# Attention with batch normalisation: x and output channel-major, the last load cut in three, one weight load on ScalarE's queue

## The reference, cut to what matters

```python
q, k, v = (einsum('oc,bchw->bohw', W, x).reshape(16, 8, 16, 256) for W in (Wq, Wk, Wv))
k = softmax(k, axis=-2)                          # over the 16 channels of a head
context = einsum('bhdn,bhen->bhde', k, v)
out = einsum('bhdn,bhde->bhen', q, context).reshape(16, 128, 16, 16)
y = einsum('oc,bchw->bohw', Wo, out) + x
mean, var = y.mean((0, 2, 3)), y.var((0, 2, 3))  # per channel, over all images
return (y - mean) * rsqrt(var + 1e-5) * gamma + beta
```

## Time and profile before

| | |
|---|---|
| Median of 3 runs | 53.73 us (52.9 to 54.81) |
| Span of the profiled execution, first to last instruction | 51.0 us |
| The median over that span | 2.7 us more |
| Busy: TensorE, VectorE, ScalarE, GpSimd | 37.5, 34.3, 27.2, 18.6 us |
| HBM read, written | 2.36 MB, 2.10 MB |

### The profile page before, as it was taken

The page is one execution under the profiler, slowest core; times in us unless marked ns, Lnnn a source line. Parts: engine busy times, 40 slices in busy tenths (PEclk is TensorE's granted clock), DMA queues, the critical chain, the costliest instruction groups (busy, mean ns, idle before and its releaser), DMA issues.

```text
span 51.0 us, 1103 instructions
## 1 busy us (share of the span) xinstructions
PE 37.5 (74%) x377; PEld 32.5 (64%) x377; DVE 34.3 (67%) x90; ACT 27.2 (53%) x61; POOL 18.6 (37%) x28
## 2 busy tenths in 40 slices
PE   3999997892789799999999999999999700000000
PEld 3999996681877498888888979797969600000000
DVE  0028699923999986994996799763764989991000
ACT  3633918509799991494386179827246926500000
POOL 5820075974994989843016008180000000000000
PEclk9999999999999999999999999999999999995555
DMA  0499999700000000000000000000000000599993
GB/s 0 121 217 360 242 295 366 241 11 0 0 0 13 0 0 0 0 6 0 0 13 6 0 0 0 0 0 13 0 0 0 0 0 0 170 338 337 343 343 113
DMA packets 4741, 4.52 MB, mean 89 GB/s; under 512 B 384, under 2 KB 4736, under 8 KB 4736
## 3 DMA queue, kind: packets, MB, share of 16 engines
q1 hardware_dynamic: 4736, 4.46, 27.7%
HBM read 2.36 MB, written 2.10 MB: 87 GB/s over the span
## 4 chain that ended last, share of the span: by engine, by line
PE 47%; DVE 16%; DMA 14%; SPq 6%; issue 3%; ACT 2%; DVEq 1%; ACTq 0%
DMA x_sb<-x_dram 14%; PE banks L505 10%; PE banks L432 9%; PE banks L472 9%; PE banks L457 8%; PE banks L489 7%; DVE y_sb L413 6%; SPq L218 4%; PE banks L486 3%; DVE stats L386 3%; DVE k_max L341 3%; DVE k_sum L354 1%; ACT x_hi L282 1%; SPq L222 1%; DVEq L64 1%
## 5 line engine op out<-in xcount | busy, mean ns | idle before, releaser
L269 POOL TENSOR_TENSOR probs<-probs,k_inv 128x256 f32<-128x256 f32 (+1 forms) x11 | 8.9, 823 | 9.2 <-DVE k_inv L360 9.2
L261 POOL TENSOR_TENSOR x_lo<-x_sb,x_hi 128x512 fp32r<-128x512 f32 (+1 forms) x7 | 7.9, 1129 | 5.5 <-ACT x_hi L282 5.5
L432 PE MATMUL banks<-wkv_hi,x_hi 128*128 128x256 f32 x32 | 7.2, 309 | 1.4 <-ACT v_sb L293 1.4
L282 ACT ACTIVATE x_hi<-x_sb 128x256 fp32r<-128x256 f32 (+1 forms) x11 | 5.4, 512 | 5.3 <-DMA x_sb<-x_dram 5.2
L341 DVE TENSOR_REDUCE k_max<-banks 128x16 f32<-128x256 f32 (+1 forms) x11 | 5.7, 529 | 1.8 <-PE banks L432 1.7
L354 DVE TENSOR_REDUCE k_sum<-probs 128x16 f32<-128x256 f32 (+1 forms) x11 | 5.6, 531 | 1.8 <-ACT probs L287 1.8
L303 ACT ACTIVATE a_hi<-banks 128x256 fp32r<-128x256 f32 (+1 forms) x9 | 3.3, 362 | 6.6 <-PE banks L489 6.6
L432 PE MATMUL banks<-wkv_hi,x_lo 128*128 128x256 f32 x32 | 6.5, 284 | 0.3 <-POOL x_lo L261 0.3
L432 PE MATMUL banks<-wkv_lo,x_hi 128*128 128x256 f32 x32 | 6.5, 287 | 0.0
L432 PEld LDWEIGHTS banks<-wkv_hi,x_hi 128*128 128x128 f32 x32 | 5.0, 196 | 2.2 <-ACT x_hi L282 1.5
L472 PE MATMUL banks<-w_sb,ct_sb 64*64 64x128 f32 x64 | 5.2, 281 | 0.5 <-DVE ct_sb L368 0.5
(11 more groups left out here) (42 smaller groups left out, 57.7 us busy)
## 6 DMA issues: line engine op xcount, KB each, us to landing
x_sb<-x_dram SPq DMA_DIRECT2D x1, 1024.0 KB, 7.1
out_dram<-y_sb SPq DMA_DIRECT2D x2, 512.0 KB, 3.5
x_sb<-x_dram SPq DMA_DIRECT2D x3, 256.0 KB, 3.2
out_dram<-y_sb SPq DMA_DIRECT2D x3, 256.0 KB, 3.5
x_sb<-x_dram SPq DMA_DIRECT2D x2, 128.0 KB, 2.2
w_sb<-w_dram SPq DMA_DIRECT2D x2, 128.0 KB, 3.0
out_dram<-y_sb SPq DMA_DIRECT2D x2, 128.0 KB, 2.0
gamma_beta<-affine_dram SPq DMA_DIRECT2D x1, 1.0 KB, 6.8
```

Of the source, the lines that this page charges most:

```text
L261: nc.gpsimd.tensor_tensor(x_lo[:, p, px], x_sb[:, p, px], x_hi[:, p, px].bitcast(F32), ALU.subtract).then_inc(x_lo_ready, hi - lo)
L269: nc.gpsimd.tensor_tensor(heads, heads, inv.to_broadcast([128, (hi - lo) * CH * HEADS, D]), ALU.mult).then_inc(probs_ready, hi - lo)
L282: nc.scalar.activation(x_hi[:, p, px], x_sb[:, p, px], ACT.Copy).then_inc(x_hi_ready, hi - lo)
L432: last = nc.tensor.matmul(kv_ps(p)[:, g, :], xs[:, p, g * 128:(g + 1) * 128], ws[:, :], start=start and g == CH * image, stop=stop, skip_g ...
```

## The change

In DRAM, x and the output become (channel, image, position); the host transposes them before and after. A load of several images is then one contiguous row for each channel: 2 KiB for two images, 4 KiB for four, and rows of one load lie 16 KiB apart. The same holds for the stores. The load of images 8 to 15 becomes (8,10), (10,12) and (12,16), each with a semaphore of its own. The key/value weights are issued by ScalarE, as the first instruction of its program, and the query/output weights behind the fifth load of x. No instruction that computes is changed.

```diff
-        x_landed = [sem(f"x_landed{i}") for i in range(6)]
+        x_landed = [sem(f"x_landed{i}") for i in range(8)]
...
-        PIECES = [(0, 1), (1, 2), (2, 4), (4, 6), (6, 8), (8, 16)]
+        PIECES = [(0, 1), (1, 2), (2, 4), (4, 6), (6, 8), (8, 10), (10, 12), (12, 16)]
...
             for i, (lo, hi) in enumerate(PIECES):
-                sp.dma_start(x_view[:, lo:hi, :], x[lo:hi].rearrange("b c n -> c b n")).then_inc(x_landed[i], 16)
-                if i == 0:
-                    sp.dma_start(w_sb[:, 0:2 * C], w[:, 0:2 * C]).then_inc(wkv_landed, 16)
-                if i == 3:
+                sp.dma_start(x_view[:, lo:hi, :], x[:, lo:hi, :]).then_inc(x_landed[i], 16)
+                if i == 4:
                     sp.dma_start(w_sb[:, 2 * C:4 * C], w[:, 2 * C:4 * C]).then_inc(wqo_landed, 16)
...
-                sp.dma_start(out[lo:hi].rearrange("b c n -> c b n"), y_view[:, lo:hi, :]).then_inc(stored, 16)
+                sp.dma_start(out[:, lo:hi, :], y_view[:, lo:hi, :]).then_inc(stored, 16)
...
         @block.scalar
         def _(act):
+            act.dma_start(w_sb[:, 0:2 * C], w[:, 0:2 * C]).then_inc(wkv_landed, 16)
...
-        "x_dram": np.ascontiguousarray(x).reshape(B, C, N),
+        "x_dram": np.ascontiguousarray(x.reshape(B, C, N).transpose(1, 0, 2)),
...
-    args.append(nc.dram_tensor("out_dram", (B, C, N), F32, kind="ExternalOutput").ap())
+    args.append(nc.dram_tensor("out_dram", (C, B, N), F32, kind="ExternalOutput").ap())
...
-    return result.results[0]["out_dram"].reshape(shape)
+    return result.results[0]["out_dram"].transpose(1, 0, 2).reshape(shape)
```

## The result

The changed kernel takes 50.89 us (median of 4 runs, 50.75 to 51.0) where the kernel before took 53.31 (4 runs, 52.87 to 54.81). The ratio is 0.958, with a 95% interval of 0.950 to 0.967: 2.2 us faster (1.8 to 2.7). The profiled execution took 51.0 us with a span of 49.3, so 1.7 us lie around the span.

What follows compares the result with a forecast made beforehand. Loads bound the front (one late load of images 8 to 15), TensorE the middle, VectorE's last outputs and stores the end. 1.6 + 0.5 + 0.5 = 2.6 us off 53.73 gives 51.1, range 50.1 to 52.8.

Steps and rivals of the forecast that it cites:

- The stages: Whole kernel: loads, TensorE run, stores have different limits; the 25 us between 17.14 and 42.5 carry over unchanged.
- The split, 1.6: Front: ScalarE's wait for images 8 and 9 goes, they land at 9.05 at the latest; TensorE run starts 1.6 us earlier.
- The issues that move, 0.5: Early loads: the third load, issued 0.47 us sooner, moves VectorE's k_max row by 0.3 to 0.7; 0.5 us taken.
- The stores, 0.5: End of the kernel: wider rows in memory make the bare stores faster, near 381 GB/s, gaining 0.5 us.
- Rival 1: Stores: wide rows gain nothing, the engines write at 340 GB/s whatever the row; 51.6 us, chance 0.15.
- rival 4: Loads and stores: rows 16 KiB apart are served badly by HBM, for instance 230 GB/s; 55.5 us, chance 0.06.
- estimate of 0.3: Stores: from a fixed cost of about 3 cycles a packet beside 1 for 32 bytes, a gain of some 0.3 us.
- 3: Front: ScalarE's weight load goes behind its table load, TensorE starts 0.83 later, the 0.5 is gone; 51.7 us, chance 0.05.
- 5: Loads: each pays a fixed cost one after another, last images at 15.7, eating the front's 2.1; 53.5 us, chance 0.01.
- rival 2: Front: another wait replaces the sixth load's, about 0.9 of the front and some store gain left; 52.6 us, chance 0.13.
- a first VectorE cast later than 3.5: Start of the kernel: a sign of being wrong; the weights were expected to land at 3.0 to 3.4.
- a remaining wait for images 8 and 9: Front, ScalarE: a sign of being wrong; no wait for data past 7.5 us was expected.

Runs made afterwards that it cites:

- layout_only: The kernel before with only x and the output channel-major: 51.94 us, ratio 0.990 (0.976 to 1.004).
- weights_only: The kernel before with only the key/value weights on ScalarE's queue and the query/output weights behind the fifth load: 53.28 us, ratio 1.015 (1.002 to 1.027).
- store_layout_only: The kernel before with only the output channel-major: 51.97 us, ratio 0.971 (0.959 to 0.984).
- split_only: The kernel before with only the last load cut in three: 51.64 us, ratio 0.981 (0.971 to 0.991).
- changed_again: The changed kernel as it is, measured once more: 50.67 us (6 runs), ratio 0.964 (0.956 to 0.973) against the kernel before.
- no_layout: The changed kernel with the image-major layout of before, keeping split and moved weights: 51.90 us, ratio 0.988 (0.974 to 1.002) against the kernel before.
- weights_back: The changed kernel with both weight loads back on SyncE, behind the first and fourth load: 51.02 us, ratio 0.959 (0.948 to 0.969) against the kernel before.
- split_in_two: The changed kernel with the last eight images in two loads, (8,10) and (10,16): 50.89 us, ratio 0.969 (0.960 to 0.977) against the kernel before.
- gamma_on_scalar: weights_back with gamma and beta issued first by ScalarE: 51.51 us, ratio 0.979 (0.968 to 0.990) against the kernel before.
- wider_pitch: The changed kernel with the rows of x 17 KiB apart in place of 16: 51.16 us, ratio 0.959 (0.952 to 0.966) against the kernel before.
- earlier_image: weights_back with images 2 and 3 loaded singly and the query/output weights behind (8,10): 50.94 us, ratio 0.968 (0.959 to 0.977) against the kernel before.
- split_store_layout: The kernel before with the split and the output channel-major, x image-major, weights on SyncE: 50.98 us, ratio 0.952 (0.940 to 0.964).
- third comparison: changed_again, split_in_two, gamma_on_scalar and earlier_image, measured beside the kernel before on the same chip: 53.50 us for the kernel before (11 runs).

## Why the prediction was right, and where its steps were not

**The stages.** In the four profiled kernels without the split, the first store issue comes a fixed time after ScalarE takes up the last load: 42.95 - 11.36 = 31.59 before. The same two rows in layout_only, weights_only (its 12.43 is above) and store_layout_only:

```profile
11.48 0.63 ACT L282 ACTIVATE x_hi<-x_sb 128x512 fp32r<-128x512 f32 x1 [0.82 <-DMA x_sb<-x_dram]
```

```profile
43.06 4.01 SPq L234 DMA_DIRECT2D out_dram<-y_sb  x7
```

```profile
44.02 4.40 SPq L232 DMA_DIRECT2D out_dram<-y_sb  x7
```

```profile
11.69 0.63 ACT L282 ACTIVATE x_hi<-x_sb 128x512 fp32r<-128x512 f32 x1 [2.14 <-DMA x_sb<-x_dram]
```

```profile
43.28 4.00 SPq L234 DMA_DIRECT2D out_dram<-y_sb  x7
```

43.06 - 11.48 = 31.58, 44.02 - 12.43 = 31.59, 43.28 - 11.69 = 31.59. So the whole front hung on that one landing, and what the prediction carried over unchanged is unchanged. With the split, the same holds in most profiles for VectorE's first k_max: split_only and changed_again show

```profile
6.88 0.75 DVE L341 TENSOR_REDUCE k_max<-banks 128x16 f32<-128x256 f32 x2
```

```profile
41.83 4.40 SPq L234 DMA_DIRECT2D out_dram<-y_sb  x7
```

```profile
41.76 4.02 SPq L232 DMA_DIRECT2D out_dram<-y_sb  x7
```

41.83 - 6.88 = 34.95 and 41.76 - 6.82 = 34.94; no_layout, weights_back, split_in_two, gamma_on_scalar and wider_pitch give 34.94 to 34.98. So in seven of the ten profiles with the split the bound is the third load, which k_max stands behind. The other three are later than that rule. In the changed kernel's first profile it is 42.02 - 6.70 = 35.32 and in earlier_image 41.76 - 6.08 = 35.68; there GpSimd's first x_lo (8.14 and 7.89), which waits for images 4 and 5, sets the front, and the first store issue comes 33.88 and 33.87 after it. In split_store_layout it is 41.42 - 6.26 = 35.16, and ScalarE waits 1.43 there for images 6 and 7; that this is the reason is not shown. So the earlier k_max of earlier_image gained nothing.

**The split, 1.6.** Right in kind, and in size as far as the scatter lets one say. Before, k_max stood at 6.27; 6.27 + 34.95 = 41.22 against 42.95 makes 1.73, if nothing but the last load's wait had gone. In split_only's own profile k_max stood at 6.88 and the first store issue came 42.95 - 41.83 = 1.12 earlier. It measured 1.77 by the medians and 1.0 (0.5 to 1.6) by the ratio. The landing of images 8 and 9 was reckoned for "9.05 at the latest", and changed_again waits until 9.78 for them; it cost nothing there, since k_max still sets the front (34.94). split_in_two bears out that the rest of the old load was covered. The kernel before also scatters more: its spans that count in the ratios lie at 50.3 to 51.9, those of the changed kernel (ten executions) at 48.6 to 49.3. The 31.59 says how it can: each microsecond of that landing is a microsecond of the time, and in the four profiles without the split ScalarE takes that load up between 11.36 and 12.43. The landings of the other executions were not profiled, so that this is the whole scatter is argued, not shown.

**The issues that move, 0.5.** This is the step that failed. It took for granted that "with that load 0.47 us sooner the row moves by 0.3 to 0.7". k_max started at 6.70 and 6.82 in the changed kernel, 0.4 to 0.6 later than 6.27. Six profiles with both weight loads on SyncE and gamma behind show images 2 and 3 taken up at 5.14, 5.75, 5.75, 5.86, 5.95 and 5.13; six with the key/value weights on ScalarE at 5.57, 5.61, 5.88, 5.97, 5.69 and 5.36. Their means are 5.60 and 5.68: an issue 0.47 us earlier brought nothing that shows. The k_max row follows: 6.27, 6.88, 6.88, 6.99, 7.08 and 6.26, mean 6.73, against 6.70, 6.74, 7.01, 7.10, 6.82 and 6.48, mean 6.81. Both differences have a standard error of 0.17, which rules out the 0.5, though not a gain of 0.2. The term was mis-sized: 0.5 forecast, -0.1 measured. A reason that fits, argued only: the same bytes, two images and the key/value weights, still stand ahead of images 2 and 3, whichever queue they come by. What did change is the start: the first image at 2.85 to 3.14 with SyncE alone, at 3.48 to 3.88 with the weights beside it, and the weights at 3.42 to 3.75 against 3.65 to 4.06. The prediction named this ("at 3.46 at worst if the first image and they now share the engines") but gave the weights too good a worst case. In the changed execution k_max is 0.43 later than in the profile of before (6.70 against 6.27), and GpSimd's late x_lo adds 42.02 - 6.70 - 34.95 = 0.37. The 0.43 is not the price of the moved issues: 6.27 is one of the two earliest of its six, and the other four are later than 6.70. The Trainium skill ("DMA: Bandwidth & Descriptors", Issuing engines are not separate DMA queues) says that issuing from several engines saves the sequencer's issue time only; here that time bought nothing that shows (5.68 against 5.60), and the first data came later.

**The stores, 0.5.** Right in kind, too small: 0.77 in the changed kernel, 0.81 and 0.83 in layout_only and store_layout_only. The prediction took its value from the best load window, 381 GB/s; the stores reached 386 to 423 in three whole slices. Rival 1, a ceiling at 340, is refuted. So is rival 4, since these stores have rows 16 KiB apart, and padding the loads' rows brought nothing. The estimate of 0.3 that the prediction works out from the Trainium skill ("DMA: Bandwidth & Descriptors", Why small descriptors are slow) was too low here, beside 0.77 to 0.83.

**The sum and the base.** For the pair of profiles: 1.73 - 0.43 - 0.37 + 0.77 = 1.70, where 2.6 was forecast; by the ratio the gain is 2.2. The time nevertheless came out at 50.89 against 51.1, because of a second error of the other sign: "the median 53.73 is 2.7 above it, and I let that stand for what lies around". What lies around a span is 1.7 to 1.9 (51.0 - 49.3 for the changed kernel, 52.38 - 50.5 for a run of before). The rest of the 2.7, 0.8 to 1.0, was that the profiled execution of before was quicker than the median of those three runs, which scatter by 1.9. So the 2.6 was reckoned on a quick execution and taken off the median of others. Against the medians it is close, 53.31 - 50.89 = 2.4 here and 53.50 - 50.67 = 2.8 in the third comparison, though its terms are not: over all profiles the first store issue is at 42.95 to 44.02 without the split (four, mean 43.3) and at 41.42 to 42.81 with it (ten, mean 41.9), so 1.4 came from the front where 2.1 were forecast, and 0.8 from the stores where it was 0.5. That the total fits so well is in part luck.

**The rivals.** 3 did not happen: ScalarE's weight load is at 0.80 and its table load behind it at 1.23. 5 is refuted by split_only; the 2 us for each transfer that the prediction names from the Trainium skill ("DMA: Bandwidth & Descriptors", Anatomy of one DMA) are a fit for transfers issued by GpSimd, and here SyncE and ScalarE issue them all. 2 came true in part: the front gave 0.93 in that execution, as rival 2 had it, by the early loads; it does not hold for every execution, since in changed_again the front gave 42.95 - 41.76 = 1.19, and the 52.6 did not come.

**Signs and slips.** Two of the prediction's signs of being wrong came: "a first VectorE cast later than 3.5" (3.76), which pointed at the term that failed, and in changed_again "a remaining wait for images 8 and 9" (0.56), which cost nothing. VectorE's sums of pair 1 came at 11.41 and not at 10.1. Two sums of its working are off: an end at 49.2 would be a gain of 51.0 - 49.2 = 1.8 from the stores and not 1.5, and rival 2's 52.6 lies 2.1% below 53.73, just outside the 2% that it is put within.

**What stays open.** Why the engines stand at a share of 0.56 with loads outstanding, and why the first image comes late when a second queue is in use, whether by the bytes or by the queue itself. No version beat the changed kernel beyond the scatter; split_store_layout and weights_back reach the same time with less changed.

## What to carry to other kernels

When an engine waits for a large load whose first part is all it needs next, cut that part off, and only that part; look in program order at what stands behind the wait. An earlier issue need not be an earlier landing while the DMA engines already have work (here 5.68 against 5.60 with 0.47 us of head start): price it at zero until a trace shows otherwise. A profile is one execution: before taking its landings as the base, ask how much of the time hangs on a single landing, and take what lies around the span from an execution that has both numbers.

## What the runs showed of the hardware that was not expected

- Packets of 1 KiB were stored at 337 to 343 GB/s in full slices; 1, 2 and 4 KiB mixed at 386 to 423 in the last three full slices of the changed kernel and at 389 to 411 in those of store_layout_only, behind a first one of 333 and 334. By the queue rows, over loads and stores together, a packet took on average 0.277 x 51.0 x 16 / 4736 = 48 ns before and 0.250 x 49.3 x 16 / 2448 = 81 ns after, for 942 and 1769 bytes. The loads as a whole did not get faster: 224 to 363 GB/s in slices 2 to 7. But where the engines were fully busy wide rows moved more there too: 422 GB/s from 8.5 to 9.0 us at a share of 1.05, against 369 in the same window and at the same share before.
- One transfer of 1 KB with rows of 8 bytes, issued first on a second queue, came with a third load 0.9 us later (6.74 against 5.86 in weights_back) and a time 0.8 us above the changed kernel's on the same chip.
- Loads with rows 16 KiB apart cost nothing against 17 KiB: images 2 and 3 at 5.86 and 5.97, 51.02 and 51.16 us on the same chip, the second with the moved weights too.
